# A reordered first layer, and a join that takes work from the experts, in a two-layer gated cross-attention kernel

## The reference

```
x = x + tanh(g_xattn[0]) * cross_attention_0(layernorm(x), ctx)          # 16 heads of 16
x = x + tanh(g_ffn[0])   * mixture_of_experts(layernorm(x))              # 64 experts, 8 of them per token,
                                                                         #   plus a shared expert for every token
x = x + tanh(g_xattn[1]) * cross_attention_1(layernorm(x), ctx, mask)
x = x + tanh(g_ffn[1])   * quantised_ffn(layernorm(x))                   # int8-like rounding by global maxima
```

## Time and profile before

| | |
|---|---|
| time, three runs | 1948.71, 1950.88 (median), 1951.15 us |
| profiled execution | 1948.85 us, its span 1947.1 us |
| busy share of the span | TensorE 89%, VectorE 71%, ScalarE 61%, GpSimd 31% |
| mean granted TensorE clock | 0.971 of full speed |
| first attention, join, experts | about 14 to 655, 655 to 691, 691 to 1223 us |
| DMA | mean 127 GB/s; 202 to 210 GB/s in the middle of the experts |

### The profile page before, as it was taken

One profiled execution on the slowest core, in us unless ns is written; L12 is line 12 of the kernel. 1 busy time (PEld: TensorE's weight loads), 2 busy tenths in 40 slices (PEclk: granted clock), 3 DMA queues, 4 the chain that ended last, 5 costly groups with the idle time before them and its releaser, 6 DMA issues.

```text
span 1947.1 us, 54303 instructions
## 1 busy us (share of the span) xinstructions
PE 1737.9 (89%) x20208; PEld 1337.4 (69%) x20208; DVE 1383.9 (71%) x4587; ACT 1179.3 (61%) x2411; POOL 610.8 (31%) x616
## 2 busy tenths in 40 slices
PE   6999999999999489999999999499999999978855
PEld 4777777777777268888888887377777777743334
DVE  4788888888888545654444443478888888859988
ACT  3777777777777223332222222388888888858875
POOL 1000000000000046766666665322222222211147
PEclk8999999999999789999999999699999999989989
DMA  3222223222224368888878875422233232203265
GB/s 99 73 90 90 90 90 98 90 90 90 90 90 145 111 179 210 209 209 203 200 202 202 203 194 121 101 90 91 87 94 90 91 93 87 81 26 154 106 236 196
DMA packets 231348, 247.63 MB, mean 127 GB/s; under 512 B 29680, under 2 KB 207216, under 8 KB 228912
## 3 DMA queue, kind: packets, MB, share of 16 engines
q1 hardware_dynamic: 206272, 205.54, 32.8%
q0 software_dynamic: 24816, 38.62, 10.9%
HBM read 142.40 MB, written 101.66 MB: 125 GB/s over the span
## 4 chain that ended last, share of the span: by engine, by line
PE 58%; DVE 23%; ACT 8%; issue 6%; POOL 2%; DMA 2%; SPq 1%; POOLq 0%; DVEq 0%; ACTq 0%
DVE mt L800 8%; PE tiles L384 7%; PE tiles L367 7%; PE bank L449 6%; ACT pt L582 6%; PE bank L1310 4%; PE tiles L1285 4%; PE bank L412 3%; PE bank L460 3%; PE tiles L351 3%; PE bank L479 3%; DVE hmax L1731 3%; PE bank L1253 2%; PE bank L1320 2%; DVE h_ring L1724 2%
## 5 line engine op out<-in xcount | busy, mean ns | idle before, releaser
L1991 POOL TENSOR_TENSOR rstd<-var,minus_half 128x2 f32<-128x2 f32 x139 | 97.0, 698 | 756.8 <-DVE var L879 743.6
L800 DVE TENSOR_REDUCE mt<-tiles 128x16 f32<-128x2048 f32 x128 | 293.5, 2293 | 28.8 <-PE tiles L367 28.3
L582 ACT ACTIVATE pt<-tiles 128x2048 f32<-128x2048 f32 x128 | 240.7, 1881 | 49.4 <-PE tiles L384 49.4
L1516 POOL DMA_INDIRECT accumulator<-ye,tid x128 | 208.4, 1629 | 154.3 <-DVE ye L1449 134.5
L1449 DVE TENSOR_SCALAR ye<-bank,xr 128x256 f32<-128x256 f32 x128 | 56.1, 480 | 248.9 <-PE bank L1297 116.5
L1501 POOL DMA_INDIRECT xr<-token_rows,tid x128 | 137.0, 1070 | 71.2 <-issue 38.5
L449 PE MATMUL bank<-xt,w_q 128*128 128x128 f32 x1024 | 155.2, 285 | 0.9 <-ACT xt L590 0.9
L367 PE MATMUL tiles<-qkp 32*128 32x256 f32 x2048 | 150.1, 406 | 3.3 <-ACT qkp L604 3.0
L384 PE MATMUL tiles<-qm,qkp 32*128 32x128 f32 x4096 | 151.1, 284 | 1.5 <-DVE mt L800 1.5
L449 PEld LDWEIGHTS bank<-xt,w_q 128*128 128x128 f32 x1024 | 132.1, 195 | 14.5 <-issue 12.9
L412 PE MATMUL bank<-pt,vx 128*32 128x128 f32 x4096 | 139.2, 277 | 2.7 <-ACT pt L582 1.7
(11 more groups left out here) (247 smaller groups left out, 4073.5 us busy)
## 6 DMA issues: line engine op xcount, KB each, us to landing
keys_values<-res SPq DMA_DIRECT2D x64, 256.0 KB
cxax<-accumulator SPq DMA_DIRECT2D x128, 128.0 KB, 2.3
cxax<-keys_values SPq DMA_DIRECT2D x128, 128.0 KB, 2.5
hidden_away<-h_ring SPq DMA_DIRECT2D x8, 1536.0 KB, 5.1
token_rows<-pay SPq DMA_DIRECT2D x64, 160.0 KB, 1.8
pt<-in_expert_up SPq DMA_DIRECT2D x36, 256.0 KB
cxax<-in_ctx SPq DMA_DIRECT2D x64, 128.0 KB, 2.2
res<-in_x SPq DMA_DIRECT2D x64, 128.0 KB, 2.3
```

Source lines behind the costliest of these rows:

```text
L582: nc.scalar.activation(pt[r % 2][:, :, :], tiles[:, :, :], ACT.Exp).then_inc(sem("exp_done"), 1)
L800: nc.vector.tensor_reduce(mt[:, :].rearrange("p (i n c) -> p i n c", i=RT, n=2 * KC)[:, :, :, 0], tiles[:, :, :].rearrange("p i (n k) -> p ...
L1516: nc.gpsimd.indirect_dma_start(out=acc[p][:, :], out_offset=bass.IndirectOffsetOnAxis(ap=tid[b % 8][:, h:h + 1], axis=0), in_=ye[r][:, h, ...
```

## The change

Three parts. In the first layer's loop, `project_v` goes ahead of `heads_to_tokens` and `moe_logits` ahead of `transposes`; from slot 65 on `moe_logits` goes ahead of `moe_counts`, and `router_tanh` follows on ScalarE. In the last slots of phase 2 the next weights' loads are issued from within the slots, and the first six keys and values products are made and stored, with ScalarE's own queue issuing their transfers. In phase 3 the places are given by two tables, `PAIR_AT` and `SHARED_AT`: 58 products stay in the slots that do not end in 5, and the shared expert of batches 0 and 1 moves to slots -2 and -1, which leaves slots 20 and 50 without one.

```diff
+        KV_EARLY = 6
+        def pair_products(pe, n, bk):
+            j = n // 2
+            if n == 0:
+                pe.wait_ge(sem("w_in"), 16 * 16)
+            pe.wait_ge(sem(f"pair_in{j % 4}"), 8 * (j - j % 4) + 32)
+            for k in range(2):
+                for c in range(KC):
...
+                    last = nc.tensor.matmul(bk[:, k * D:(k + 1) * D], weights_, moving, start=(c == 0), stop=(c == KC - 1))
+            last.then_inc(sem("kv_done"), 1)
+
+        def early_pairs(stage):
+
+            if stage(5) is not None and stage(5)[0] == NB - 1:
+                return range(0, 2)
+            if stage(6) is not None and stage(6)[0] == NB - 1:
+                return range(2, KV_EARLY)
+            return ()
...
                 scores(m)
                 if L == 0:
+                    if m is None:
+                        moe_logits(v)
                     moe_counts(u)
+                    project_v(f)
                     heads_to_tokens(o)
-                    project_v(f)
+                    if m is not None:
+                        moe_logits(v)
                     transposes(f)
-                    moe_logits(v)
                     scores_t(k)
...
                     values(k)
+                    for n in early_pairs(stage):
+                        pe.wait_ge(sem("exp_done"), NB)
+                        wait(pe, "kv_out", n - 1)
+                        pair_products(pe, n, bank[n % 2])
...
                     normalise_first(f)
+                    if m is None:
+                        router_tanh(v)
                     copy_counts(u)
                     copy_v(f)
                     normalise_second(w)
+                    if m is not None:
+                        router_tanh(v)
                     copy_xt(f)
-                    router_tanh(v)
...
                     copy_ov(k)
+                    for n in early_pairs(stage):
+                        p = n % 2
+                        act.wait_ge(sem("kv_done"), n + 1)
+                        act.wait_ge(sem(f"x3_kept{p}"), 8 * ROOM_TO)
+                        wait(act, f"kv_kept{p}", 8 * (n - p))
+                        nc.scalar.copy(kvs[p], bank[p][:, :]).then_inc(sem("kv_out"), 1)
+                        act.wait_ge(sem("kv_out"), n + 1)
+                        act.dma_start(keys_values[n], kvs[p]).then_inc(sem(f"kv_kept{p}"), 16)
+                        if p == 1:
+                            load_pair(act, n // 2 + 4)
...
                     load(stage(-2))
+                    if stage(4) is not None and stage(4)[0] == NB - 1:
+                        sp.wait_ge(sem("o_done_0"), NB)
+                        attention_weights(sp, 1, "w_in")
...
                     store_transposed(stage(5))
+                    if stage(5) is not None and stage(5)[0] == NB - 1:
+                        sp.wait_ge(sem("pv_done"), NB)
+                        first_expert_weights(sp, EARLY_FREE, 4)
                     store_row(stage(5))
...
             if L == 0:
+                first_expert_weights(sp, 4, WEIGHT_BUFFERS)
                 load_steps((NB - 1, (NB - 1) % 4))
...
+        PAIR_AT = numbered(KV_EARLY, [s for s in range(E) if s % 10 != 5])
+        SHARED_AT = numbered(0, [-2, -1] + [s for s in range(E) if s not in (20, 50)])
...
-            def body(stage):
+            def body(s, stage):
                 slot_steps(stage(-MAP_AHEAD))
                 rows_t(stage(0))
-                keys_or_values(stage(0))
-                shared_down(stage(1))
+                keys_or_values(PAIR_AT.get(s))
+                shared_down(SHARED_AT.get(s - 1))
                 up(stage(1))
-                shared_up(stage(0))
+                shared_up(SHARED_AT.get(s))
                 down(stage(2))
...
             attention_sp(sp, 0)
-            sp.wait_ge(sem("o_done_0"), NB)
-            attention_weights(sp, 1, "w_in")
-            sp.wait_ge(sem("pv_done"), NB)
-            first_expert_weights(sp)
```

More of the change, by code:

```diff
@@ L1149, in expert_slots, with numbered @@
         def expert_slots(body):
-            slots(body, E, -MAP_AHEAD, E + 2)
+            for s in range(-MAP_AHEAD, E + 2):
+                body(s, lambda lag, s=s: (s - lag, (s - lag) % 4) if 0 <= s - lag < E else None)
+        def numbered(first, places):
+            return {s: (first + k, (first + k) % 4) for k, s in enumerate(places)}
+        PAIR_AT = numbered(KV_EARLY, [s for s in range(E) if s % 10 != 5])
+        SHARED_AT = numbered(0, [-2, -1] + [s for s in range(E) if s not in (20, 50)])
+        assert max(PAIR_AT.values())[0] == E - 1 and max(SHARED_AT.values())[0] == NB - 1
         def expert_of(n):
@@ L1164, in expert_weights, with first_expert_weights @@
             sp.dma_start(wc[k], a["L0_ffn_w2"][one].rearrange("o f d -> f (o d)")).then_inc(sem(name), 16)
-        def first_expert_weights(sp):
-            for b in range(EARLY_FREE, WEIGHT_BUFFERS):
+        def first_expert_weights(sp, first, last):
+            for b in range(first, last):
                 expert_weights(sp, b, "e_w_first")
@@ L1240, in keys_or_values @@
                     return
-                n, _ = e
-                j = n // 2
-                if n == 0:
-                    pe.wait_ge(sem("w_in"), 16 * 16)
-                pe.wait_ge(sem(f"pair_in{j % 4}"), 8 * (j - j % 4) + 32)
-                wait(pe, "kv_out", n)
-                for k in range(2):
-                    for c in range(KC):
-                        if n % 2 == 0:
-                            weights_, moving = w_k[:, c, k * P:(k + 1) * P], cxp[j % 4][:, c, :, :].rearrange("p e t -> p (e t)")
-                        else:
-                            weights_, moving = cxp[j % 4][:, c, k, :], w_v[:, c, :]
-                        last = nc.tensor.matmul(bank[5][:, k * D:(k + 1) * D], weights_, moving, start=(c == 0), stop=(c == KC - 1))
-                last.then_inc(sem("kv_done"), 1)
+                wait(pe, "kv_out", e[0])
+                pair_products(pe, e[0], bank[5])
             weights = weights_pe(pe)
@@ L1379, in shared_out, with body @@
                 nc.scalar.activation(ys[n % 2], bank[7][:, 0:D], ACT.Copy, scale=tg_half[:, 0:1]).then_inc(sem("sh_out"), 1)
-            def body(stage):
+            def body(s, stage):
                 copy_t(stage(0))
-                copy_pair(stage(0))
-                shared_out(stage(1))
+                copy_pair(PAIR_AT.get(s))
+                shared_out(SHARED_AT.get(s - 1))
                 gate_tanh(stage(1))
-                shared_tanh(stage(0))
+                shared_tanh(SHARED_AT.get(s))
                 if stage(0) is not None and stage(0)[0] in WEIGHTS_AT:
```

18 lines of the change are left out of this document (11 added, 7 removed).

## The result

| | before | after |
|---|---|---|
| median, us | 1951.02 (1948.71 to 1952.06, 4 runs) | 1938.91 (1938.06 to 1939.10, 4 runs) |
| ratio to before | | 0.9939, 95% from 0.9922 to 0.9956 |
| profiled execution: time, span | 1948.85, 1947.1 | 1938.06, 1936.2 |

The kernel became 12 us faster, where 24 were forecast; 1938.9 lies outside the range of 1915 to 1936. The sign was right and the size was half.

The account below looks back on a forecast made before the run. Bounds: a hole in each first-layer slot, a join where nearly everybody waits, and an expert loop over two engines. From 1948.85, -20.9 - 2.3 + 0.5 = -22.7 gives 1926.1, placed at 1927, range 1915 to 1936.

Parts of the forecast that it names:

- The loop: First layer's loop: reordering hides the values' copy until the maximum limits, 0.36 us in each of 58 slots, 20.9 gained.
- The join: Between first layer and experts: the experts' first matmul starts at 679.2 in place of 681.48, 2.3 us gained.
- Each needs the buffer of the one two before it stored (2.2 to 3 us): Join, ScalarE: products 2 to 5 wait for buffer stores, two such rounds with eight issues, ending near 678.8.
- the forecast's 663.5: Join: time when layer 1's weights have landed, the last load taking 3 us; products 0 and 1 wait for it.
- The bound for SyncE's chain alone: Join: with free issues on ScalarE and weights landed at 662, it ends at 676.5, 5 us gained.
- The 0.5 for each of ScalarE's issues: Join: time assumed for each DMA issue on ScalarE, taken from SyncE's since no row showed one.
- The rule that I set aside: Join: skill's rule that several issuers save only sequencer time, making moved issues worth little; the forecast held the rows disagreed.
- The ramp: Start of experts: with shared experts 0 and 1 first, slot 0 starts 16.3 us after the join, not 9.7; 6.6 late.
- What slots 20 and 50 give back: Expert slots 20, 21, 50 and 51: without those two shared experts they are together 6.1 us shorter.
- Slots without a product: Expert slots 5, 15, ..., 55: as long as their neighbours, since VectorE still holds `shared_down`; gain 0, other end 10.4.
- I take 0: Expert slots 5, 15, ..., 55: gain assumed from six omitted products of 1.73 us each, VectorE being the cover.
- the early work is in the way: Rival, join and experts' ramp: late weights and low clock lose 1 and 3 us, giving 1932; chance 0.12.

Follow-up runs that it names:

- e2: The changed kernel with the first layer's loop middle back in the old order, all join and expert changes kept: 1956.25 us, ratio 1.0043.
- e10: e5 with slot 61's burst of loads spread over five slots and the last table's read back issued ahead of the last six expert loads: ratio 0.9864.
- e11: e10 with shared experts 0 and 1 moved as in the change, their tokens' loads issued ahead of the eight mask loads: ratio 0.9866.
- e12: The changed kernel with all waits and issues, but ScalarE's early transfers carrying a quarter of the bytes: ratio 0.9923.
- e5: The changed kernel without early products and with shared experts in their old slots, leaving the order and the loads issued within slots: ratio 0.9888.
- e3: The changed kernel without the six early keys and values products, all 64 made in the expert slots: ratio 0.9902.
- e9: The changed kernel with six different buffers for the six early products, so ScalarE never waits for a store before copying: ratio 0.9938.
- e6: The changed kernel with only products 0 and 1 early, slots 15 and 25 without a product: ratio 0.9904.
- e1: The kernel before with only the first layer's order changed; weights' loads, products and shared experts as before: 1926.82 us, ratio 0.9894.
- e4: The changed kernel with the shared experts back in their old slots, none in -2 and -1: ratio 0.9938.
- e7: The changed kernel with slots 15, 21, 25, 35, 45 and 51 without a product in place of 5, 15, ..., 55: ratio 0.9916.

## Why the prediction was half right

**The loop: right.** The hole went, the maximum is the next limit, 9.36 for 9.34. The term had 58 slots at 0.36, 20.9. From the 3rd second pass to the 61st the traces show 19.2 over 58 slots: 0.35 in 54 of them, less in the first two, and nothing in two that stay at 9.71. From the 62nd pass to the 63rd nothing comes (9.29 before, in e2 and in the change).

**Slot 61: not in the sum.** I counted the freed room's burst as part of an even loop. Over an even slot it costs 1.3 before (10.96 - 9.70) and 1.8 to 4.1 in the kernels with the order, and nothing when it is spread (e10, e11). Of the 2.4 between 13.48 in the change and 11.11 in e12, 1.2 are a longer wait for the store (3.12 and 1.90), and the rest goes with the low clock behind it (a mean of 0.87 in the slot, 1.00 in e12). The two stores land 4.17 and 3.26 after their issue; what sets that stays open.

**The join: the step that failed.** "Each needs the buffer of the one two before it stored (2.2 to 3 us)" is the time of a load in a quiet stretch. On the chain the stores took 3.7 and 5.5. The reading back of the last table, 2.8 in the forecast (675.2 to 678), takes 3.10 in e5, 4.08 in e3 and 5.90 in e9. No term asked what the DMA engines would have to do: six stores of 256 KB, six `ctx` loads of 128 KB, and the expert loads pulled into the same 10 us. Removing the bytes shortened the waits (e12), removing the waits alone exposed the next transfer (e9). Of the 5.9 us that the products cost (e3), products 2 to 5 are 4.0 (e6), and the other 1.95 come with products 0 and 1, ahead of the counts. Set beside the forecast's own times, the join is 5.0 late in two parts. The counts came 33.1 behind the 63rd pass, for 31.0: product 0 began 26.6 behind that pass, where the forecast's 663.5 is 25.5 behind it, and the two products took 6.5, not 5.5, at granted clocks of 0.50 and 0.61. That is 2.1; the other 2.9 come behind the counts, in ScalarE's waits for its stores. The bound for SyncE's chain alone was too good as well: 676.5 is 38.5 behind the 63rd pass, and e3 and e5, which have that chain alone, take 40.2 and 40.8. The 0.5 for each of ScalarE's issues was 0.34 to 0.36 for a store and 0.5 for a load, some 0.9 less over six stores, an estimate.

The rule that I set aside ahead of the run deserved more. The Trainium skill ("DMA: Bandwidth & Descriptors", Issuing engines are not separate DMA queues) says that transfers started by several engines run on the same 16 DMA engines and interleave, and that another issuer saves only issue time. This case agrees: 0.35 of issue beside transfers of 3.7 to 5.9 us, at a DMA share of 1.0. The loads moved into the slots brought 0.8 us of join (e1 to e5), of the 10.6 us that 21 issues take in the kernel before: a table's store of 16 KB went from 1.87 to 4.09 us and came 4.4 later.

**The ramp: right, 6.8 for 6.6,** partly by luck: against its own twin (e4) the move costs 8.1, and 1.4 come from the other parts. The chain was as described, load, `shared_up`, tanh, `shared_down`, copy, `shared_up`. Loads issued earlier are worth 1.1 to 1.4 and not 3.7 (e11).

**What slots 20 and 50 give back: right.** Slots 20, 21, 50 and 51 are 5.8 shorter than before, for 6.1. Slot 3 is 0.37 longer, which the forecast had not.

**Slots without a product: right but for one.** Slots 15, 25, 35, 45 and 55 are as long as before to 0.02. Slot 5 is not:

```profile
721.50 0.66 PE L1313 MATMUL tiles<-ident,xr 128*128 128x128 f32 x4
724.09 1.13 PE L1366 MATMUL bank<-w_sd,res 128*128 128x256 f32 x4 [1.94 <-DVE res L1506]
725.06 3.44 PE L1331 MATMUL tiles<-xrt,pt 128*128 128x256 f32 x8
...
731.43 0.66 PE L1313 MATMUL tiles<-ident,xr 128*128 128x128 f32 x4
```

It lasts 9.93 in place of 8.24: after the hole the up products run at a granted clock of 0.53, 3.44 for 1.89. "I take 0" had VectorE as cover for the hole itself, rightly, and left out that a hole in TensorE's work can be followed by the low clock.

Of the rivals, "the early work is in the way" came nearest in place (the join loses, the experts' ramp loses), but its 1932 had late weights and the clock as cause, and 1 us for the join where 2.7 were lost. At 0.12 it had too small a chance, and the range left out that effects without a price, the stores and slot 61, could add up.

## What to carry to other kernels

Before work is moved into an idle stretch of the compute engines, add up the bytes that it and its neighbours will move there, and compare with what the DMA engines moved per us in the busiest row: a latency read in a quiet stretch does not hold in a full one. A burst of loads stands in the queue ahead of every store behind it: 13 issues made the store of slot 61 9.4 us late and cost a wait of 1.2 to 3.2, and one part a slot cost nothing. And test the parts alone: one part carried the gain, and the others took 9 to 12 us of it.

## What had not been expected

- **A small transfer on busy DMA engines takes as long as a large one.** The 16 KB of the last table took 5.90 us at a share of 1.03 (e9), 3.10 in e5 at 0.68; the 256 KB stores of the change took 3.7 and 5.5.
- **Places without a product are fine until the clock falls, and where it falls moves.** The penalty is 1.6 to 1.7 us a slot: slot 5 in the change, e2, e9 and e12, slot 15 in e6, slots 15, 25 and 35 in e7, slot 35 in e4. The others with the same hole don't show it. In the change slot 15's hole before L1366 is 1.54 and the up products behind it take 1.89:

```profile
807.60 1.13 PE L1366 MATMUL bank<-w_sd,res 128*128 128x256 f32 x4 [1.54 <-DVE res L1506]
808.57 1.89 PE L1331 MATMUL tiles<-xrt,wlast 128*128 128x256 f32 x8
```

  Slot 5's was 1.94. The length of the hole alone doesn't settle it: slots 15, 25 and 35 have holes of 1.54, 1.87 and 1.87 in e7 and in the change alike, and are cold in the one and warm in the other. What does stays open. Each such hole is a chance of losing 1.7.
- **Order of issue matters less than the end of the queue's work.** Moving the read back ahead of six loads (e10) changed J by 0.2 us, less than the scatter between executions.
